# First expert scaled on its own by sums of squares in a macaron block

## The reference

```python
x = x + 0.5 * ffn(layernorm(x))            # 8 experts, FFN = 512
x = x + linear_attention(layernorm(x))     # 16 heads of 8
x = x + 0.5 * ffn(layernorm(x))
# ffn: for each of the 8 experts, all summed
#   h = silu(x @ wg) * (x @ wu);  acc = acc + h @ wd
```

## Time and profile before

| | us |
|---|---|
| median of 3 runs (2050.87 to 2051.57) | 2051.28 |
| the profiled execution | 2051.42 |
| its span, first to last instruction | 2049.6 |
| busy in the span: TensorE | 2043.9 |
| VectorE | 1660.2 |
| ScalarE | 1441.1 |
| GpSimd | 709.0 |

### The profile page before, as it was taken

The page is one execution under the profiler, slowest core; times in us unless marked ns, Lnnn a source line. Parts: engine busy times, 40 slices in busy tenths (PEclk is TensorE's granted clock), DMA queues, the critical chain, the costliest instruction groups (busy, mean ns, idle before and its releaser), DMA issues.

```text
span 2049.6 us, 29729 instructions
## 1 busy us (share of the span) xinstructions
PE 2043.9 (100%) x9598; PEld 936.0 (46%) x9599; DVE 1660.2 (81%) x2749; ACT 1441.1 (70%) x2508; POOL 709.0 (35%) x718
## 2 busy tenths in 40 slices
PE   9999999999999999999999999999999999999999
PEld 5444444444444444444444444444444444444445
DVE  7886787878787878787878787878787878877776
ACT  7777767767776676677766776676667766666665
POOL 6631134334423432335234323523344233430000
PEclk9999999999999999999999999999999999999999
DMA  7031246244633543556245333543255446522101
GB/s 216 16 51 17 70 102 138 53 103 87 137 88 77 109 89 73 91 105 130 58 88 109 73 98 81 105 94 98 68 108 125 93 72 131 114 37 42 21 11 27
DMA packets 251565, 174.42 MB, mean 85 GB/s; under 512 B 164881, under 2 KB 221713, under 8 KB 251409
## 3 DMA queue, kind: packets, MB, share of 16 engines
q1 hardware_dynamic: 215744, 129.47, 27.0%
q0 software_dynamic: 35520, 43.00, 13.2%
q10 hardware_dynamic: 144, 0.07, 0.0%
HBM read 99.88 MB, written 30.93 MB: 64 GB/s over the span
## 4 chain that ended last, share of the span: by engine, by line
PE 97%; DVE 1%; DMA 1%; POOL 0%; ACT 0%; issue 0%; SPq 0%; DVEq 0%; ACTq 0%; POOLq 0%
PE bank L647 11%; PE bank L648 11%; PE bank L654 11%; PE bank L670 11%; PE bank L666 11%; PE bank L667 11%; PE bank L699 10%; PE bank L695 10%; PE bank L696 10%; PE bank L716 1%; PE bank L714 1%; PE bank L715 1%; DMA turn_scratch<-turn_sb 0%; DMA arena<-in_L_ffn_Wu 0%; DVE h_lo L997 0%
## 5 line engine op out<-in xcount | busy, mean ns | idle before, releaser
L794 ACT ACTIVATE silu_sb<-bank,scal 128x512 f32<-128x512 f32 x1024 | 704.7, 688 | 572.5 <-PE bank L654 562.8
L990 DVE SCALAR_TENSOR_TENSOR bank<-silu_sb,scal,bank 128x512 f32<-128x512 f32 x976 | 732.4, 750 | 365.1 <-ACT silu_sb L794 360.1
L997 DVE TENSOR_TENSOR h_lo<-bank,h_hi 128x512 f16<-128x512 f32 x976 | 668.6, 685 | 0.1
L801 ACT ACTIVATE h_hi<-bank 128x512 f16<-128x512 f32 x976 | 577.5, 592 | 3.3 <-DVE bank L990 3.0
L647 PE MATMUL bank<-xn,wg_hi 128*128 128x512 f16 x1024 | 388.1, 379 | 0.7 <-ACT wg_hi L784 0.7
L666 PE MATMUL bank<-xn,wu_hi 128*128 128x512 f16 x1024 | 388.2, 379 | 0.3 <-DVE h_lo L997 0.2
L670 PE MATMUL bank<-xn,wu_lo 128*128 128x512 f16 x1024 | 388.1, 379 | 0.3 <-POOL wu_lo L1168 0.3
L667 PE MATMUL bank<-xn,wu_hi 128*128 128x512 f16 x1024 | 388.1, 379 | 0.0
L648 PE MATMUL bank<-xn,wg_hi 128*128 128x512 f16 x1024 | 388.1, 379 | 0.0
L654 PE MATMUL bank<-xn,wg_lo 128*128 128x512 f16 x1024 | 387.8, 379 | 0.0
L699 PE MATMUL bank<-h_hi,wd_lo 128*128 128x512 f16 x1012 | 383.6, 379 | 0.0
(11 more groups left out here) (124 smaller groups left out, 1428.0 us busy)
## 6 DMA issues: line engine op xcount, KB each, us to landing
arena<-rep_scratch SPq DMA_DIRECT2D x128, 512.0 KB, 6.9
arena<-arena POOLq DMA_DIRECT2D x56, 512.0 KB, 4.9
turn_scratch<-turn_sb SPq DMA_DIRECT2D x208, 64.0 KB, 1.9
x_tok<-turn_scratch POOLq DMA_DIRECT2D x52, 256.0 KB, 4.9
rep_scratch<-arena SPq DMA_DIRECT2D x16, 512.0 KB, 2.7
x_tok<-in_L_attn_x SPq DMA_DIRECT2D x16, 256.0 KB, 5.4
term_scratch<-arena SPq DMA_DIRECT2D x8, 512.0 KB, 3.4
arena<-term_scratch SPq DMA_DIRECT2D x8, 512.0 KB, 3.9
```

The costliest lines, as they stand in the source:

```text
L794: act.activation(silu_sb[:, n % 3, :], gate_ps[n % NG][:, :], ACT.Silu, scale=unscale[G[group(n)]]).then_inc(sem("silu"), 1)
L990: dve.scalar_tensor_tensor(up_ps[n % NUP][:, :] if n >= NF else h_sb(n), silu_sb[:, n % 3, :], (h_scale if n >= N_ALL else h_first)[group(n)],
L997: dve.tensor_tensor(h_lo[:, n % NH, :], up_ps[n % NUP][:, :], h_hi[:, n % NH, :], ALU.subtract).then_inc(sem("h_lo"), 1)
```

## The change

The first expert becomes a scale group alone: the groups are experts 0, 1, 2 to 3 and 4 to 7, so the first pass over the weights has four parts for each of the two blocks instead of three, with one more evacuation of down results each. The first loads bring one expert (256 KB) where they brought two, and block 1 is loaded straight after block 0; blocks 2 to 15 are loaded later, from a table.

For wg, wu and wd of expert 0 and wg and wu of expert 1 the scale comes from a sum of squares in place of a maximum: ScalarE squares the 512 columns and adds them up in one instruction (`square`), TensorE adds over the partitions with a product of one column (`spread`), and three instructions of VectorE on one column make the scale (`root_power`, `root_unscale`, `root_scale`). For the other groups the diagonal goes too: TensorE multiplies the row maxima by an identity. VectorE writes the high parts of wg and wd of expert 0, and normalizes half of block 0 and half of block 1; GpSimd keeps only the power step. The first three units of TensorE are written out in `firsts`.

```diff
-    CUTS = (0, NC // NP, 2 * NC // NP, NC)
+    CUTS = (0, SL, 2 * SL, 4 * SL, NC)
...
+    WARM = (12, 1, 1)
+    SPREADS = [(5, 4), (11, 5), (25, 6)]
+    LATE = {("g", 1): 3, ("u", 1): 4, ("d", 1): 9, ("g", 2): 12, ("u", 2): 13, ("g", 3): 15, ("u", 3): 16, ("d", 2): 17}
...
+    for blk in range(2, NB):
+        sp_at[24 + 2 * blk].append(("x", blk))
...
+        PIECES = [(0, 1), (1, 2), (2, 4), (4, 6), (6, 8)]
...
-            for w in range(2):
+            load_x(1)
+            for w in range(3):
                 load_w(w, 0)
-            load_x(1)
-            load_w(2, 0)
-            for i in range(1, NP):
+            for i in range(1, len(PIECES)):
                 for w in range(3):
...
             def spread(i):
-                pe.wait_ge(sem("w_diag"), i + 1)
+                k, m = SPREAD[i]
+                if i < NROOT:
+                    pe.wait_ge(sem("w_square"), k + m)
+                elif i < NROOT + 2:
+                    pe.wait_ge(sem("w_max"), 3 * (i - NROOT) + 1)
+                else:
+                    pe.wait_ge(sem("w_row"), 1)
                 take_turn("spread", i)
-                m = SPREAD[i][1]
-                pe.matmul(misc_ps[:, 0:m * P], ones_half[:, :], max_diag[:, 0:m, :].rearrange("p m q -> p (m q)"),
-                          start=True, stop=True).then_inc(sem("spread"), 1)
+                for j in range(m):
+                    if i < NROOT:
+                        made = pe.matmul(misc_ps[:, j:j + 1], ones_half[:, :], amax_row[k + j].bitcast(BF16)[:, 1:2], start=True, stop=True)
+                        continue
+                    made = pe.matmul(misc_ps[:, cols(j, P)], top_half(k + j), ident_half[:, :], start=True, stop=True)
+                made.then_inc(sem("spread"), 1)
 
 
             def norm_T(s):
                 if s:
                     pe.wait_ge(sem("lo_first"), 1)
-                    pe.wait_ge(sem("norm_second"), 1)
-                else:
-                    pe.wait_ge(sem("norm"), TT)
-                for t in range(TT):
+                    pe.wait_ge(sem("norm_second"), 2)
+                    pe.wait_ge(sem("norm_late"), 4)
+                for t in (2, 3, 0, 1):
+                    if s == 0:
+                        pe.wait_ge(sem(("norm", "norm_late")[t // 2]), t % 2 + 1)
                     made = pe.transpose(down_ps[:, cols(t, P)], xn_tok[:, 0, cols(t, P)], ident[:, :])
                 made.then_inc(sem("norm_T"), 1)
+
+            def firsts():
+                pe.wait_ge(sem("xn_hi"), 1)
+                for n in range(NG):
+                    if n == 0:
+                        pe.wait_ge(sem("wg_first"), 1)
+                    elif n == NG - 1:
+                        pe.wait_ge(sem("wg_hi"), 1)
+                    pe.matmul(gate_ps[n][:, :], wg_hi[:, cols(n, P)], xn_hi[:, 0, :], start=True, stop=False)
+                pe.wait_ge(sem("wg_lo"), 1)
+                for n in range(NG):
+                    pe.matmul(gate_ps[n][:, :], wg_lo[:, cols(n, P)], xn_hi[:, 0, :], start=False, stop=False)
+                spread(2)
+                pe.wait_ge(sem("lo_first"), 1)
+                for n in range(NG):
+                    pe.matmul(gate_ps[n][:, :], wg_hi[:, cols(n, P)], xn_lo[:, 0, :], start=False, stop=True).then_inc(sem("gate"), 1)
+                pe.wait_ge(sem("wu_hi"), 1)
+                for n in range(NG):
+                    pe.matmul(up_ps[n][:, :], wu_hi[:, cols(n, P)], xn_hi[:, 0, :], start=True, stop=False)
+                    pe.matmul(up_ps[n][:, :], wu_hi[:, cols(n, P)], xn_lo[:, 0, :], start=False, stop=False)
+                norm_T(1)
+                pe.wait_ge(sem("wu_lo"), 1)
+                for n in range(NG):
+                    pe.matmul(up_ps[n][:, :], wu_lo[:, cols(n, P)], xn_hi[:, 0, :], start=False, stop=True).then_inc(sem("up"), 1)
+                spread(3)
 
...
             idle(WARM[0])
             pe.wait_ge(sem("pool_const"), 1)
-            pe.wait_ge(sem("pool_ones"), 1)
+            spread(0)
+            idle(WARM[1])
             norm_T(0)
-            idle(WARM[1])
-            spread(0)
+            spread(1)
             idle(WARM[2])
-            for n in range(NG):
-                gate_high(n)
-            for n in range(NG):
-                gate_low(n)
+            firsts()
...
+            def less_mean(k):
+                act.wait_ge(sem("mean_var"), k + 1)
+                act.activation(shift[:, k, :], mean_var[:, k, :, 0], ACT.Copy, scale=-1.0).then_inc(sem("less_mean"), 1)
...
+            def square(j):
+                x, w = divmod(j, 3)
+                act.wait_ge(sem(f"w{w}_in{x}"), 16)
+                if j:
+                    act.wait_ge(sem("w_square"), j)
+                act.activation(down_sb[:, :], raw_of[w][:, cols(x, FF)], ACT.Square, scale=2.0 ** -SQUARE_EXP,
+                               accum_out=amax_row[j]).then_inc(sem("w_square"), 1)
...
+            less_mean(0)
+            square(G[0])
             act.wait_ge(sem("shift"), 1)
-            for t in range(TT):
+            for t in range(2):
                 norm(0, t, 0, "norm")
+            square(U[0])
             act.wait_ge(sem("norm_T"), 1)
             act.activation(xn_hi[:, 0, :], down_ps[:, :], ACT.Copy).then_inc(sem("xn_hi"), 1)
-            weight_high("g", wg_hi, raw_g, G, 0)
+            square(DN[0])
+            less_mean(1)
             weight_high("u", wu_hi, raw_u, U, 0)
+            square(G[1])
+            square(U[1])
+            act.wait_ge(sem("shift"), 2)
+            for t in range(2):
+                norm(1, t, 1, "norm_second")
...
+            def norm_eps(blk):
+                dve.wait_ge(sem("mean_var"), blk + 1)
+                dve.tensor_scalar(var_eps[:, blk, :], mean_var[:, blk, :, 1], LN_EPS, None, ALU.add).then_inc(sem("eps_lead"), 1)
+
+            def norm_shift(blk):
+                dve.wait_ge(sem("rstd_lead"), blk + 1)
+                dve.wait_ge(sem("less_mean"), blk + 1)
+                dve.tensor_tensor(shift[:, blk, :], shift[:, blk, :], rstd[:, blk, :], ALU.mult).then_inc(sem("shift"), 1)
+
+            def norm_late(blk):
+                if blk:
+                    dve.wait_ge(sem("norm_T"), 1)
+                for t in range(2, TT):
+                    dve.tensor_scalar(xn_tok[:, 0, cols(t, P)], x_tok[:, blk * TT + t, :], mean_var[:, blk, t, 0:1],
+                                      rstd[:, blk, t:t + 1], ALU.subtract, ALU.mult).then_inc(sem("norm_late"), 1)
+
...
+            def root_power(i):
+                k, m = SPREAD[i]
+                dve.wait_ge(sem("spread"), i + 1)
+                for j in range(m):
+                    made = dve.tensor_scalar(pow2[k + j].bitcast(I32), misc_ps[:, j:j + 1].bitcast(I32), 24, 23,
+                                             ALU.logical_shift_right, ALU.logical_shift_left)
+                made.then_inc(sem("root_power"), 1)
+
+            def root_unscale(i):
+                k, m = SPREAD[i]
+                dve.wait_ge(sem("root_power"), i + 1)
                 for j in range(k, k + m):
+                    made = dve.tensor_scalar(unscale[j], pow2[j], 2.0 ** -124, 2.0 ** (64 + SQUARE_EXP - F_EXP), ALU.max, ALU.mult)
+                made.then_inc(sem("root_unscale"), 1)
+
+            def root_scale(i):
+                k, m = SPREAD[i]
+                dve.wait_ge(sem("root_unscale"), i + 1)
+                dve.reciprocal(cells(3, k, m), cells(4, k, m)).then_inc(sem("w_scale"), 1)
...
+            norm_eps(0)
             dve.wait_ge(sem("x_in1"), 16)
             norm_stats(1, 1, "stats")
             norm_aggr(1, "stats", 2, "mean_var")
+            norm_shift(0)
+            norm_late(0)
+            for step in (root_power, root_unscale, root_scale):
+                step(0)
+            dve.wait_ge(sem("w_scale"), 1)
+            for half, made in ((0, "wg_first"), (1, "wg_hi")):
+                j = cols(half, FF // 2)
+                dve.tensor_scalar(wg_hi[:, j], raw_g[:, j], scale[G[0]], None, ALU.mult).then_inc(sem(made), 1)
+            root_power(1)
+            dve.wait_ge(sem("wg_first"), 1)
+            weight_low("g", wg_hi, wg_lo, raw_g, G, 0)
+            root_unscale(1)
+            norm_eps(1)
+            root_scale(1)
             dve.wait_ge(sem("xn_hi"), 1)
             dve.tensor_tensor(xn_lo[:, 0, :], down_ps[:, :], xn_hi[:, 0, :], ALU.subtract).then_inc(sem("lo_first"), 1)
-            weight_scale(0)
+            root_power(2)
+            weight_low("u", wu_hi, wu_lo, raw_u, U, 0)
+            norm_shift(1)
+            root_unscale(2)
+            norm_late(1)
+            root_scale(2)
             group_scales(0)
-            weight_low("g", wg_hi, wg_lo, raw_g, G, 0)
-            weight_low("u", wu_hi, wu_lo, raw_u, U, 0)
-            piece_max(2, 0, amax_row[DN[0]])
+            dve.wait_ge(sem("w_scale"), 3)
+            dve.tensor_scalar(wd_hi[:, cols(0)], raw_d[:, cols(0)], scale[DN[0]], None, ALU.mult).then_inc(sem("wd_hi"), 1)
```

(40 more changed lines are left out.)

147 lines of the change are left out of this document (72 added, 75 removed).

## The result

The changed kernel takes 2057.61 us (median of 7 runs, 2056.34 to 2058.42) against 2051.53 us for the kernel before beside it: the ratio is 1.0028, with an interval of 1.0019 to 1.0038. It is slower by 6 us, where 3.8 us less was forecast. The profiled execution took 2057.61 us, with a span of 2055.8.

The account below looks back on a forecast made before the run. TensorE bounds the kernel: start of the first product, products end to end, few waits, an unchanged tail. Unit 8 comes 4.0 us earlier, less 0.2: 2051.42 − 3.8 = 2047.6, or 2047.5 us against the median; range 2046.8 to 2049.4.

Parts of the forecast that it names:

- The lead-in: Kernel start up to unit 8: first product at 8.75 us instead of 13.02, unit 8 at 23.1 instead of 27.14.
- 0.2 of it was taken off by judgement: Margins of 0.1 to 0.2 us at units 3 to 7: 0.2 off the 4.0 us gain, leaving 3.8.
- the landing of wg: First loads: wg of expert 0 lands at 5.63 us, since the bytes up to its end stay the same.
- From the landing to the first product: Lead-in: from wg landing at 5.63 us, through squares, tiles, transposes and `xn_hi`, to the first product at 8.75.
- The square with its sum: ScalarE's new instruction over 512 columns, shown by no row: between 0.72 and 0.93 us, taken as 0.80.
- The wait before the second transposes: TensorE before block 1's transposes: waits 0.7 us behind two squares and two tiles on ScalarE, starting them at 12.85.
- The rests of expert 1's wg and wu: VectorE before unit 8: 0.77 us each, written by about 21.7 us, costing nothing as unit 8 starts at 23.1.
- the count of slow matmuls of ones: TensorE's first 44 matmuls of ones: 25 were slow, at 0.22 us against 0.11, the rate rising at about 6.8 us.
- case (a): Rival, first products at the low clock: 0.43 us each, gain 1.1 to 1.3 us, time about 2050.1; chance 0.15.
- the two more evacuations and turns: First pass: they lie in ScalarE's and VectorE's free time and cost nothing.
- from unit 60 on, each engine's list is the old one: Kernel behind the first pass: every engine's work is unchanged from unit 60 on.
- (d): Rival, slower: the clock stays low into the dense stage; slower by 0.2% needs 16 us of it, 2055.5 us; chance 0.03.

## Why the prediction was wrong

**The lead-in was right, and its terms nearly so.** Forecast were 8.75 us for the first product and 23.1 for unit 8; measured were 9.12 and 23.32, with 3.8 us gained at that point as taken, and with the transfers early the whole kernel takes 2047.73 us where 2047.5 was forecast. That the sum hit 3.8 so closely is in part luck: 0.2 of it was taken off by judgement, and the landing of wg alone varies from 6.23 to 6.72 us over seven traces with one order of loads. Unit 8 follows it by 16.8 us in each of them that has the ones and single squares.

Several terms were off and partly cancelled. Wg landed not at 5.63 but at 6.48, though the sum of bytes up to its end was the same (768 KB, or 0.79 MB), so these bytes alone don't set a landing. By 6.48 us 1.24 MB had moved (192 GB/s over 6.48 us), so loads issued later took part of the rate. From the landing to the first product the prediction had 3.12 us, and it took 2.64. ScalarE's tiles stood behind its square, and so behind the landing, as these rows of the changed kernel show:

```profile
6.48 0.63 ACT L847 ACTIVATE down_sb<-arena 128x512 f32<-128x512 f32 x1 [1.17 <-DMA arena<-in_L_ffn_Wg]
7.02 0.19 ACT L847 ACTIVATION_READ_ACCUMULATOR down_sb<-arena 128x1 f32 x1
7.11 0.87 ACT L825 ACTIVATE xn_tok<-x_tok,shift,rstd 128x128 f32<-128x128 f32 x2
```

The square with its sum is an activation of 0.63 us and a read of the sum of 0.19, some 0.73 in all (6.48 to 7.21): inside the bounds of 0.72 and 0.93, at their lower end. The wait before the second transposes was 0.3 instead of 0.7 us: TensorE came there 0.4 us later than forecast (12.55 instead of 12.15), the transposes only 0.15 (13.00 instead of 12.85). The rests of expert 1's wg and wu took VectorE 1.60 and 1.12 us where 0.77 each was taken, and ended at 23.02 instead of 21.7, 0.3 us ahead of unit 8. And the count of slow matmuls of ones does not follow from its own 0.11 and 0.22 us: they give 23 and a rise at 6.4 us, not 25 and 6.8.

**The clock held.** The products run 0.216 us apart from the start in the changed kernel, so case (a) did not occur there. The runs without ones and with doubled squares show that it was near. The rate rises at different times in the executions: the same 24 matmuls of ones took 5.49 us in the changed kernel and 5.23, 4.71 and 4.62 us in the versions with early transfers, with wg first and with doubled squares. Nor does the length of a gap decide alone whether the clock falls. Gaps of 0.9 us and 1.4 us before the first product left the full level, and so did the 2.59 us near 139 us; the gap of 1.8 us with doubled squares lost it (0.50 from 8.6 us on), and so did 4.74 us at 116 us, which cost another 2.9. The Trainium skill ("TensorE: Matmul & The Clock Gate", Part 1) has the low clock as the default that comes back with idleness. The traces agree in the direction: each low stretch shown here behind the first rise follows a gap.

**The step that failed** is the one that costs "the two more evacuations and turns" at nothing and ends with "from unit 60 on, each engine's list is the old one". It named ScalarE's and VectorE's free time, and left out what each part issues on GpSimd's queue: one accumulating transfer, 4.9 to 5.2 us each in a chain. With two of them more, the second long wait comes (2.6 us, or 9.6 where the first is absent). The change also moves them, from `NF + 2 * e` to `NF + e`, so that three instead of two stand ahead of block 2's norm, which brings the first (4.7 us and 2.9 at the low clock). The parts and the kernel before stood in the text ahead; the moved line is not in the part of the diff shown there, and the prediction speaks of neither. None of the rivals was this mechanism: the slower one, (d), was a clock that stays low.

**The trace of before showed that there was little room.** Its list of waits between 90 and 160 us, which the prediction doesn't use, has both consumers waiting already:

```profile
POOL x_tok L1210 <- DMA x_tok<-turn_scratch: 8.8, 3, 3.8
...
ACT xn_tok L778 <- POOL shift L1162: 1.5, 1, 1.5
DVE stats L917 <- DMA x_tok<-turn_scratch: 0.7, 1, 0.7
```

ScalarE waits 1.5 us for block 2's shift and VectorE 0.7 for the attention's statistics; TensorE doesn't yet; that the units in flight cover this is a reading of the queues and was not tested. A list of TensorE's waits alone hides that. The chain starts when GpSimd's last `h_lo` of the first pass is done, and so moves with the lead-in: 104.81 us in the changed kernel against 108.39 before. A shorter lead-in alone thus opens no wait, as the version with five transfers shows. Seven transfers end 10 us further behind their start than five (2 x 5). One transfer more ahead of the norm was too much for TensorE in the kernel before, as the run with three shows.

**What stays open.** How much of the time behind the first product the squares alone set could not be separated from the clock in the run that doubles them. That wg's landing moved with the order of loads by more than its bytes was only seen, not tested, and what decides whether a gap lowers the clock is not shown.

## What to carry to other kernels

A part, a tile or a group more is more than its arithmetic: list everything that it issues, on every queue, and look for what stands behind it there. Transfers that each wait for the last one to land form a chain with a price of its own, and belong where the engine that issues them has slack, here in the first pass, at 0.7 us. Before calling a later stage unchanged, read the waits of all engines in it: an engine that waits there without holding up the one that bounds the kernel is a sign that the margin is small.

## What was not expected of the hardware

The granted clock reads 1.00 in two different states. In the run without ones, the stretch from 8.94 to 13.00 us reads 1.00 with products 0.42 us apart, and in the run with doubled squares and in the changed kernel at 120 us it reads 0.50 with the same spacing. The reading showed the drops, but not the low level before the first rise, so at a kernel's start the spacing of equal matmuls is the evidence. And wg of expert 0 landed at 6.23 to 6.72 us behind two blocks of x (6.48 in the changed kernel), but by 4.9 behind one: 1.3 to 1.8 us for 256 KB, about twice what the 325 GB/s of the microsecond from 3 us in the changed kernel would make (0.8).
